# A max-then-softmax attention whose key pieces are compared in pairs: the pairing extended from one third to two thirds of the pieces

## The chip, the core and the metric

The kernel runs on one core of a Trainium2 chip. The metric is the device time of one execution in microseconds. A TensorE clock of 1.00 in the profile is its full 2.4 GHz, 0.50 is 1.2 GHz.

## What is computed

Two attention layers over a 48 x 48 picture with 384 channels, batch 2, 12 heads of 32 channels. The first layer attends to a 7 x 7 neighbourhood, the second to all 2304 positions with a bias by row and by column. Cut to the second layer, which the change touches:

```python
q, k, v = (qkv[0], qkv[1], qkv[2])
q = q * scale
attn = jnp.einsum('bqd,bkd->bqk', q, k)
attn = (attn.reshape(B * nh, H, W, H, W) + rel_h[:, :, :, :, None] + rel_w[:, :, :, None, :]).reshape(B * nh, N, N)
attn = jax.nn.softmax(attn, axis=-1)
out = jnp.einsum('bqk,bkd->bqd', attn, v)
```

Before, in between and after stand the group norms, the projections and the residual sums (`x = x + layer(_gn(x))`).

## The kernel before

**Stages, units, steps.** The second attention is `attention_full`. It has 24 stages, one for each head and batch element. A stage has six units of 384 queries, and a unit has nine steps; a step takes 256 of the 2304 keys (two key tiles of 128). So a stage has 54 steps, and the whole 1296.

**Two passes.** The softmax needs the largest score of each query before the exponentials. A first pass (`max_piece` on TensorE, L1608) makes scores in half precision, with queries on the partitions: for each of a unit's three query tiles, six pieces of 384 keys. The second pass (`scores_of`, L1635 and L1637) makes the scores again with keys on the partitions, the negated maximum added as one more row of the matmul. `exps` (L1760, ScalarE) takes the exponential, `low_part` (L1796) subtracts its upper half to keep the rest as a second half-precision number, and `weighted` (L1662, L1663) multiplies both with the values. `low_part` runs on VectorE for steps 1, 4 and 7 of a unit and on GpSimd for the six others.

**Order.** Each engine runs its own list, written by hand. The first pass runs 12 steps ahead of the second (`AHEAD`): in each step TensorE makes four score matmuls, one piece (call it p0), the weighted sums of the step three before, and a second piece (p1). Two PSUM banks hold the pieces in turn, so a piece waits until the piece two before it has been read. At step 7 of a unit, ahead of the scores, `row_of_max` (L1621) turns the three negated maxima of the coming unit into a row, which `place_row` on ScalarE (L1731) copies beside the queries; it waits for the maxima, and for the reading of the next unit's first piece, since it writes into that bank.

**Rounds.** How a piece pair is read depends on the step (`is_round`). In a plain step VectorE reduces each of the two pieces to its maximum (L1817, `maxima`). In a round step the even piece's matmul gives the difference of two key pieces' scores instead of a score: the constants (`rival_m`) and the key vectors (`rivals`, L1875, on GpSimd, once a stage in step 31) hold the difference in that piece's place. ScalarE copies it with relu (`leads`, L1746), and one VectorE instruction adds the odd piece and takes the maximum over all (L1810: max(a - b, 0) + b is the larger of the two). In a round step TensorE issues p0 between the second and the third score matmul, in a plain step behind the fourth. Before, steps 2, 5 and 8 of a unit are rounds: the last two of a tile's six pieces. After nine steps VectorE reduces the parts of each tile to the negated maximum (L1824).

**Other work between.** ScalarE takes the result's lower part out of PSUM after step 2 (L1716) and writes the normalised result after step 4 (L1724); VectorE adds the two parts after step 3 (L1835, L1836).

Of the kernel before, what the change touches and what calls it, by code (L numbers as in the profile page):

```python
# [15 lines left out]
TOK = SIDE * SIDE  # L16
ALL = B * TOK
HEADS, D = 12, 32
# [15 lines left out]
UNIT = KR * SIDE  # L34
PIECE = 384
PIECES = TOK // PIECE
RIVALS = slice(TOK - 2 * PIECE, TOK - PIECE)
LOWEST = -3.0e38
QT = UNIT // 128
HALO = WINDOW // 2  # L40
# [46 lines left out]
def shape_constants():  # L87

    t = np.arange(TOK)
    strip, row, col = t // STRIP, (t % STRIP) // KC, t % KC  # L90
    one_a = np.zeros((32, TOK + REGS), np.float16)
    for i in range(KC):
        one_a[i, :TOK] = one_a[KC + i, :TOK] = col == i
    one_b = np.zeros((B_ROWS, NA + 1, 128), np.float16)
    for a in range(NA):
        for k in range(128):
            one_b[a * KR + k // KC, a, k] = one_b[SIDE + a * KR + k // KC, a, k] = 1
    one_m = np.zeros((2 * SIDE, TOK + REGS), np.float16)
    one_m[t // SIDE, t] = 1
    one_m[SIDE + t % SIDE, t] = 1  # L100
    strip_m = np.zeros_like(one_m)
    strip_m[row, t] = 1
    strip_m[SIDE + strip * KC + col, t] = 1
    rival_m = strip_m.copy()
    rival_m[:, RIVALS] -= strip_m[:, RIVALS.stop:RIVALS.stop + PIECE]
    pos = np.arange(SIDE)
    start = np.clip(pos - HALO, 0, SIDE - WINDOW)
    outside = ~((pos[:, None] >= start[None]) & (pos[:, None] < start[None] + WINDOW))
    far = np.where(outside, -BIG, 0.0).astype(np.float16)
    far_row = far[:, t // SIDE]  # L110
    far_col = far[:, t % SIDE]
    mask_a = np.zeros((32, NS, TOK), np.float16)
    for c in range(NS):
        mask_a[:KC, c] = far_col[c * KC:(c + 1) * KC]
    mask_b = np.concatenate([far_row, np.zeros_like(far_row)])
    by_strip = row * SIDE + strip * KC + col
    mask_m = np.concatenate([far_row, far_col])[:, by_strip]
    ones_row = np.zeros((B_ROWS, NA + 1, 128), np.float16)
    ones_row[M_ROW] = 1
    group = np.arange(C) // (C // GROUPS)  # L120
    share = (group[:, None] == group[None]).astype(np.float32) / (C // GROUPS)
    share = share.reshape(CT, 128, C).transpose(1, 0, 2).copy()
    spread = (np.arange(2 * HEADS)[:, None] % HEADS == np.arange(C)[None] % HEADS) / INV_SCALE
    spread = spread.astype(np.float16).reshape(2 * HEADS, CT, 128)
    big = np.float16(BIG)
    return {
        "one_a0": one_a * big, "one_a1": one_a, "one_b0": one_b * big + ones_row,
        "one_b1": one_b + ones_row, "one_m0": one_m * big, "one_m1": rival_m,
        "mask_a": mask_a, "mask_b": mask_b, "mask_m": mask_m, "share": share, "spread": spread,
        "ident": np.eye(128, dtype=np.float16),  # L130
    }
# [1266 lines left out]
def attention_full(nc, ctx, x, dram, sem):  # L1398


    PAIRS = TILES // 2
# [7 lines left out]
    STEP_PIECES = 2  # L1409
    UNIT_PIECES = STEP_PIECES * PAIRS  # L1410
    ROUNDS = PIECES // 2
    PARTS = PIECES - 1
    AHEAD = PAIRS + 3
    ROW_STEP = 7
    RIVALS_STEP = 4 * PAIRS - 5
# [71 lines left out]

    def is_round(m):

        return m % ROUNDS == ROUNDS - 1  # L1490

    def rounds(g, m):

        return g * QT + m % PAIRS // ROUNDS + 1

    def row_of(n, k):

# [20 lines left out]
    with nc.Block() as block:  # L1518
# [189 lines left out]
        @block.scalar  # L1708
        def _(act):
            def banked(a):  # L1710
                return out_acc[:, a % 2, 0:QT * VW].rearrange("p (t n) -> p t n", t=QT)

            def take_lo(n, a):

                act.wait_ge(prob_used, n * STEPS + (a + 1) * PAIRS)
                nc.scalar.activation(out_lo[:, a % 2], banked(a)[:, :, 0:D], ACT.Identity).then_inc(lo_copied, 1)  # L1716

            def normalise(h, b, a):

                act.wait_ge(sum_ready, (h * B + b) * NA + a + 1)  # L1720
                if a == 0 and due(h):
                    act.wait_ge(result_out[b], h * RESULT)
                for t in range(QT):
                    nc.scalar.activation(result[:, b, a * QT + t, :], out_sum[:, a % 2, t, :], ACT.Identity,  # L1724
                                         scale=inverse[:, a % 2, t:t + 1]).then_inc(placed, 1)


            def place_row(n, u, b):

                act.wait_ge(row_ready, n * NA + u + 1)  # L1730
                nc.scalar.activation(q_b[M_ROW:M_ROW + 1, b, u * UNIT:(u + 1) * UNIT],  # L1731
                                     max_acc[M_ROW:M_ROW + 1, u % 2, 0:UNIT], ACT.Identity).then_inc(row_copied, 1)

            act.wait_ge(first_in, FIRST)
            nc.scalar.activation(warm[:, :], ident[0:1, 0:1], ACT.Exp)
            def leads(n, m):


                u = m // PAIRS
                g = n * NA + u  # L1740
                j = 2 * (m % PAIRS)
                done = rounds(g, m)
                act.wait_ge(bank_filled, g * UNIT_PIECES + j + 1)
                if due(done - 2):
                    act.wait_ge(bank_read, (done - 3) // QT * UNIT_PIECES + ((done - 3) % QT + 1) * PIECES)
                nc.scalar.activation(lead[:, done % 2, :], max_acc[:, piece_bank(g, u, j), 0:PIECE],  # L1746
                                     ACT.Relu).then_inc(lead_ready, 1)

            for m in range(AHEAD):
                if m - AHEAD + PAIRS == ROW_STEP:  # L1750
                    place_row(0, 0, 0)
                if is_round(m):
                    leads(0, m)

            def exps(n, k):
                free = n * STEPS + k - RING + 1
                act.wait_ge(score_ready, n * STEPS + k + 1)
                if due(free):
                    act.wait_ge(prob_used, free)
                nc.scalar.activation(prob[:, (n * STEPS + k) % RING, :].rearrange("p (j n) -> p j n", j=2),  # L1760
                                     scores[:, 2 * (k % 2):2 * (k % 2) + 2, 0:UNIT], ACT.Exp).then_inc(prob_ready, 1)

            def stage(h, b):
                n = h * B + b
                for k in range(STEPS):
                    coming = row_of(n, k)
                    if coming:
                        place_row(*coming, b if coming[1] else 1 - b)
                    later = ahead(n, k)
                    if later and is_round(later[1]):  # L1770
                        leads(*later)
                    exps(n, k)
                    u, rest = divmod(k - LAG, PAIRS)
                    if rest == PAIRS - 1:
                        if u >= 0:
                            take_lo(n, u)
                        elif not is_first(n):
                            take_lo(n - 1, NA + u)
                    if rest == 1:
                        if u >= 1:  # L1780
                            normalise(h, b, u - 1)
                        elif not is_first(n):
                            normalise(h - (1 - b), 1 - b, NA - 1)

            each_stage(act, stage)
            take_lo(STAGES - 1, NA - 1)
            normalise(HEADS - 1, 1, NA - 1)
# [13 lines left out]
        def _(dve):  # L1801
            def maxima(n, m):
# [3 lines left out]
                if is_round(m):  # L1806
# [3 lines left out]
                    nc.vector.tensor_tensor_reduce(  # L1810
                        out=winner[:, done % 2, :], in0=max_acc[:, piece_bank(g, u, first + 1), 0:PIECE],
                        in1=lead[:, done % 2, :], scale=1.0, scalar=LOWEST, op0=ALU.add, op1=ALU.max,
                        accum_out=part_max[:, u % 2, first // PIECES, PARTS - 1:PARTS]).then_inc(bank_read, 2)
                else:
                    for j in range(first, first + STEP_PIECES):
                        dve.wait_ge(bank_filled, g * UNIT_PIECES + j + 1)
# [48 lines left out]
        @block.gpsimd  # L1865
        def _(pool):
            nc.gpsimd.memset(neg_max[:, :, :], 0.0).then_inc(neg_clear, 1)
            nc.gpsimd.memset(zeros[:, :], 0.0).then_inc(zeros_ready, 1)

            def rivals(h, b):  # L1870


                pool.wait_ge(max_in[b], (h + 1) * MAX)
                ours = k_m[0:D, b, RIVALS]
                nc.gpsimd.tensor_tensor(ours, ours, k_m[0:D, b, RIVALS.stop:RIVALS.stop + PIECE],  # L1875
                                        ALU.subtract).then_inc(rivals_ready, 1)

            rivals(0, 0)

            def stage(h, b):  # L1880
                n = h * B + b
                for k in range(STEPS):
                    if k == RIVALS_STEP and not is_last(n):
                        rivals(h + b, 1 - b)
                    low_part(nc.gpsimd, n, k, low_by_pool)

            each_stage(pool, stage)
# [248 lines left out]
```

## Time and profile before

| | before |
|---|---|
| median of 3 runs | 3177.81 us (3173.26 to 3178.23) |
| profiled execution, its own time | 3173.97 us |
| span of its trace | 3172.2 us |
| TensorE, weight loads, VectorE, ScalarE, GpSimd busy in the span | 2850.6, 1862.6, 2427.4, 2027.8, 1741.1 us |
| mean granted TensorE clock | 0.959 |

A profile is one execution. Durations are read from its trace, and instants are microseconds from the span's start. An instruction's start is recorded; the end of a matmul is modelled, and matmuls overlap in the pipeline, so starts say more about TensorE than busy time does. On VectorE and ScalarE the next instruction can start a little before the recorded end of the one ahead of it. An idle time is put down to the engine whose semaphore came last.

### The profile page before, as it was taken

What the parts mean: (1) busy time and instruction counts of PE and PEld (TensorE: products, weight loads), DVE (VectorE), ACT (ScalarE), POOL (GpSimd) and SP (SyncE); (2) the same over time, 40 slices, a digit from 0 to 9 for tenths busy, and PEclk for the clock granted to TensorE, in tenths of its full rate; (3) what the DMA queues carried; (4) which work ended last, traced back from release to release, by engine and by line L of the source; (5) the groups of instructions that cost most, each with busy time, mean ns of one, the idle gap of its engine ahead of it and who ended that gap; (6) DMA issues with size and microseconds to landing.
All of it is one profiled execution on the core that took longest, in us unless ns stands there. A gap on an engine that the chain in (4) does not pass through costs nothing. (4 is left out here: it accounts for less than half of the span.)

```text
span 3172.2 us, 84223 instructions
## 1 busy us (share of the span) xinstructions
PE 2850.6 (90%) x34200; PEld 1862.6 (59%) x34200; DVE 2427.4 (77%) x5315; ACT 2027.8 (64%) x3866; POOL 1741.1 (55%) x1441
## 2 busy tenths in 40 slices
PE   3895999997669974999999999999999999999977
PEld 2453777774335531666666666666666666666654
DVE  6754888785666533888888888888888888888854
ACT  3433676664334432777777777777777777777764
POOL 3452555552020021777777777777777777777762
PEclk9996999998889986999999999999999999999989
DMA  3426555555526857333332222222222223333115
GB/s 144 157 91 143 141 140 138 137 138 157 199 76 195 225 135 202 66 62 55 64 57 52 52 52 52 52 52 52 52 52 52 52 52 59 63 62 58 23 43 150
DMA packets 219847, 302.00 MB, mean 95 GB/s; under 512 B 134394, under 2 KB 172884, under 8 KB 213972
## 3 DMA queue, kind: packets, MB, share of 16 engines
q1 hardware_dynamic: 219460, 296.62, 38.4%
q8 instruction: 270, 4.42, 0.6%
q14 instruction: 117, 0.96, 0.1%
HBM read 196.56 MB, written 92.64 MB: 91 GB/s over the span
## 5 line engine op out<-in xcount | busy, mean ns | idle before, releaser
L1796 POOL TENSOR_TENSOR fprob_low<-fprob 128x768 f16<-128x768 f32 x864 | 1251.0, 1469 | 547.6 <-ACT fprob L1760 547.6
L1760 ACT ACTIVATE fprob<-fscores 128x768 f32<-128x768 f32 x1296 | 1048.6, 809 | 277.2 <-PE fscores L1637 240.2
L1817 DVE TENSOR_REDUCE fpart_max<-fmax_acc 128x1 f32<-128x384 f32 x1728 | 919.1, 557 | 240.9 <-PE fmax_acc L1608 199.2
L1608 PE MATMUL fmax_acc<-fk_m,fq_m 128*128 128x384 f16 x2592 | 845.3, 327 | 30.2 <-DMA fident<-in_ident 27.3
L1635 PE MATMUL fscores<-fq_a,fk_a 128*128 128x384 f16 x2592 | 842.1, 325 | 10.8 <-DMA fk_m<-in_one_m 10.8
L1637 PE MATMUL fscores<-fq_b,fk_b 97*128 97x384 f16 x2592 | 846.9, 327 | 0.0
L1662 PE MATMUL fout_acc<-fv,fprob 128*128 128x65 f16 x7776 | 610.4, 191 | 3.0 <-POOL fprob_low L1796 2.4
L1663 PE MATMUL fout_acc<-fv,fprob_low 128*128 128x33 f16 x7776 | 593.4, 178 | 1.2 <-issue 1.2
L1662 PEld LDWEIGHTS fout_acc<-fv,fprob 128*128 128x128 bf16 x7776 | 541.2, 97 | 90.4 <-POOL fprob_low L1796 3.7
L1663 PEld LDWEIGHTS fout_acc<-fv,fprob_low 128*128 128x128 f16 x7776 | 486.5, 96 | 78.4 <-issue 1.4
L1796 DVE TENSOR_TENSOR fprob_low<-fprob 128x768 f16<-128x768 f32 x432 | 426.4, 987 | 5.9 <-ACT fprob L1760 5.9
L1135 POOL TENSOR_TENSOR prob_low<-prob 128x242 f16<-128x242 f32 (+2 forms) x360 | 249.8, 716 | 257.6 <-ACT prob L1093 255.4
L1608 PEld LDWEIGHTS fmax_acc<-fk_m,fq_m 128*128 128x128 f16 x2592 | 251.0, 97 | 189.6 <-DVE fpart_max L1817 99.7
L1637 PEld LDWEIGHTS fscores<-fq_b,fk_b 97*128 97x128 f16 x2592 | 250.7, 97 | 162.8 <-issue 0.5
L1635 PEld LDWEIGHTS fscores<-fq_a,fk_a 128*128 128x128 f16 x2592 | 251.3, 97 | 69.2 <-DMA fk_m<-in_one_m 11.2
L1746 ACT ACTIVATE flead<-fmax_acc 128x384 f32<-128x384 f32 x432 | 210.0, 486 | 109.1 <-PE fmax_acc L1608 109.1
L1810 DVE CUSTOM_DVE_ANT_0 fwinner<-fmax_acc,flead 128x384 bf16<-128x384 f32 x432 | 240.9, 558 | 13.2 <-PE fmax_acc L1608 2.7
L1153 DVE TENSOR_REDUCE tile_max<-max_acc 128x1 f32<-128x282 f32 (+3 forms) x432 | 176.7, 436 | 77.7 <-PE max_acc L921 76.8
L1074 ACT ACTIVATE x<-out_acc 32x384 f32<-32x384 f32 (+1 forms) x288 | 138.8, 482 | 129.8 <-PE out_acc L982 126.1
L1093 ACT ACTIVATE prob<-scores 128x266 f32<-128x266 f32 (+1 forms) x576 | 188.4, 407 | 45.4 <-PE scores L943 41.4
L942 PE MATMUL scores<-q_a,k_a 128*128 128x57 f16 (+4 forms) x1296 | 175.2, 225 | 29.9 <-DMA q_b<-max_row 28.2
L470 PE MATMUL acc<-x,w_hi 128*128 128x384 f16 (+1 forms) x441 | 150.5, 343 | 56.2 <-POOL x L324 29.1
(138 smaller groups left out, 4266.4 us busy)
## 6 DMA issues: line engine op xcount, KB each, us to landing
q_a<-q_hi SPq DMA_DIRECT2D x48, 432.0 KB, 5.8
fq_a<-q_hi SPq DMA_DIRECT2D x48, 432.0 KB, 7.8
q_a<-q_lo SPq DMA_DIRECT2D x24, 432.0 KB, 7.5
row_bias<-bias_slot SPq DMA_DIRECT2D x24, 432.0 KB, 7.3
col_bias<-bias_slot SPq DMA_DIRECT2D x72, 144.0 KB, 4.8
fq_a<-q_lo SPq DMA_DIRECT2D x24, 432.0 KB, 8.7
fq_a<-col_bias SPq DMA_DIRECT2D x24, 432.0 KB, 17.0
fq_b<-row_bias SPq DMA_DIRECT2D x24, 432.0 KB, 5.8
```

Of the source, the lines that this page charges most:

```text
L1093: nc.scalar.activation(dst, src, ACT.Exp).then_inc(prob_ready, 1)
L1135: last = engine.tensor_tensor(prob_low[0:p, k % RING, cut], prob[0:p, k % RING, cut], prob[0:p, k % RING, :].bitcast(BF16)[:, 1::2][:, cut ...
L1608: nc.tensor.matmul(max_acc[:, piece_bank(g, u, j), 0:PIECE], q_m[:, b, tile * 128:(tile + 1) * 128], k_m[:, b, piece * PIECE:(piece + 1) * ...
L1635: nc.tensor.matmul(bank, k_a[:, b, tile * 128:(tile + 1) * 128], q_a[:, b, tile // NA, a * UNIT:(a + 1) * UNIT], start=True, stop=False)
L1637: last = nc.tensor.matmul(bank, k_b[:, tile % NA], q_b[:, b, a * UNIT:(a + 1) * UNIT], start=False, stop=True)
L1662: nc.tensor.matmul(dst, high[:, cut], v[:, b, tile, :], start=False, stop=False)
L1663: last = nc.tensor.matmul(dst[:, D:VW], low[:, cut], v[:, b, tile, D:VW], start=False, stop=(tile == TILES - 1 and t == QT - 1))
L1746: nc.scalar.activation(lead[:, done % 2, :], max_acc[:, piece_bank(g, u, j), 0:PIECE], ACT.Relu).then_inc(lead_ready, 1)
L1760: nc.scalar.activation(prob[:, (n * STEPS + k) % RING, :].rearrange("p (j n) -> p j n", j=2), scores[:, 2 * (k % 2):2 * (k % 2) + 2, 0:UNI ...
L1796: engine.tensor_tensor(prob_low[:, slot, :], prob[:, slot, :], prob[:, slot, :].bitcast(BF16)[:, 1::2], ALU.subtract).then_inc(done, 1)
L1810: nc.vector.tensor_tensor_reduce(out=winner[:, done % 2, :], in0=max_acc[:, piece_bank(g, u, first + 1), 0:PIECE], in1=lead[:, done % 2, : ...
L1817: nc.vector.reduce_max(part_max[:, u % 2, j // PIECES, j % PIECES:j % PIECES + 1], max_acc[:, piece_bank(g, u, j), 0:PIECE], axis=AX.X).th ...
```

## The change

In the second layer steps 1, 2, 4, 5, 7 and 8 of a unit become rounds; steps 0, 3 and 6 stay plain. Of a tile's six pieces the first two are still reduced one by one, pieces 2 and 3 and pieces 4 and 5 are compared as differences. The constants hold two difference pieces, the subtraction on GpSimd covers two pieces of 384 keys in one instruction, and a tile has four partial maxima, not five. The wait of a lead for its buffer follows the new count of rounds. The diff in full:

```diff
-RIVALS = slice(TOK - 2 * PIECE, TOK - PIECE)
+RIVALS = (2 * PIECE, 4 * PIECE)
...
     rival_m = strip_m.copy()
-    rival_m[:, RIVALS] -= strip_m[:, RIVALS.stop:RIVALS.stop + PIECE]
+    for at in RIVALS:
+        rival_m[:, at:at + PIECE] -= strip_m[:, at + PIECE:at + 2 * PIECE]
...
     ROUNDS = PIECES // 2
-    PARTS = PIECES - 1
+    PARTS = PIECES - 2
...
     def is_round(m):
 
-        return m % ROUNDS == ROUNDS - 1
+        return m % ROUNDS > 0
 
     def rounds(g, m):
 
-        return g * QT + m % PAIRS // ROUNDS + 1
+        return (g * QT + m % PAIRS // ROUNDS) * (ROUNDS - 1) + m % ROUNDS
...
                 if due(done - 2):
-                    act.wait_ge(bank_read, (done - 3) // QT * UNIT_PIECES + ((done - 3) % QT + 1) * PIECES)
+                    tiles, pair = divmod(done - 3, ROUNDS - 1)
+                    act.wait_ge(bank_read, tiles * PIECES + 2 * (pair + 2))
...
-                        accum_out=part_max[:, u % 2, first // PIECES, PARTS - 1:PARTS]).then_inc(bank_read, 2)
+                        accum_out=part_max[:, u % 2, first // PIECES, 1 + m % ROUNDS:2 + m % ROUNDS]).then_inc(bank_read, 2)
...
                 pool.wait_ge(max_in[b], (h + 1) * MAX)
-                ours = k_m[0:D, b, RIVALS]
-                nc.gpsimd.tensor_tensor(ours, ours, k_m[0:D, b, RIVALS.stop:RIVALS.stop + PIECE],
+                ours = k_m[0:D, b, RIVALS[0]:TOK].rearrange("p (i s n) -> p i s n", s=2, n=PIECE)
+                nc.gpsimd.tensor_tensor(ours[:, :, 0], ours[:, :, 0], ours[:, :, 1],
                                         ALU.subtract).then_inc(rivals_ready, 1)
```

## Rows read from the trace of the kernel before

**Rows 1.** Busy us (instructions) of PE, PEld, DVE, ACT, POOL in a stretch; clock, DMA.

```profile
1700.00:2700.00 1000.00, 979.36 (x13236) 659.89 (x13235) 879.50 (x1914) 764.38 (x1357) 711.89 (x493) 1.00 0.29 55
```

**Rows 2.** Waits, 1258 to 3040 us: waiter <- releaser: us in total, times, longest.

```profile
PE fmax_acc L1621 <- DVE fpart_max L1817: 35.1, 142, 0.4
...
PE fscores L1635 <- DMA fk_m<-in_one_m: 10.8, 1, 10.8
```

**Rows 3.** Timeline of TensorE, steps 5 to 7: start, us, line, out<-in [idle before].

```profile
2006.11 0.32 PE L1635 MATMUL fscores<-fq_a,fk_a 128*128 128x384 f16 x1
...
2006.44 0.33 PE L1608 MATMUL fmax_acc<-fk_m,fq_m 128*128 128x384 f16 x1
...
2007.27 0.32 PE L1608 MATMUL fmax_acc<-fk_m,fq_m 128*128 128x384 f16 x1
2007.43 0.32 PE L1635 MATMUL fscores<-fq_a,fk_a 128*128 128x384 f16 x1
...
2008.09 0.33 PE L1608 MATMUL fmax_acc<-fk_m,fq_m 128*128 128x384 f16 x1
...
2009.16 0.33 PE L1621 MATMUL fmax_acc<-fident,fneg_max 128*128 128x128 f16 x3 [0.25 <-DVE fpart_max L1817]
2009.32 0.33 PE L1635 MATMUL fscores<-fq_a,fk_a 128*128 128x384 f16 x1
```

**Rows 4.** Timeline of VectorE over the same steps (x2: two in a row).

```profile
2006.78 0.95 DVE L1796 TENSOR_TENSOR fprob_low<-fprob 128x768 f16<-128x768 f32 x1
2007.77 0.56 DVE L1810 CUSTOM_DVE_ANT_0 fwinner<-fmax_acc,flead 128x384 bf16<-128x384 f32 x1
...
2008.45 1.05 DVE L1817 TENSOR_REDUCE fpart_max<-fmax_acc 128x1 f32<-128x384 f32 x2
```

**Rows 5.** Timeline of ScalarE over steps 4 and 5 of that unit.

```profile
2005.65 0.81 ACT L1760 ACTIVATE fprob<-fscores 128x768 f32<-128x768 f32 x1 [0.59 <-PE fscores L1637]
2006.36 0.73 ACT L1724 ACTIVATE fresult<-fout_sum,finverse 128x32 f32<-128x32 f32 x3
2006.99 0.47 ACT L1746 ACTIVATE flead<-fmax_acc 128x384 f32<-128x384 f32 x1
2007.36 0.80 ACT L1760 ACTIVATE fprob<-fscores 128x768 f32<-128x768 f32 x1
```

**Rows 6.** Timeline of ScalarE and VectorE ahead of the first step.

```profile
1235.55 0.49 ACT L1746 ACTIVATE flead<-fmax_acc 128x384 f32<-128x384 f32 x1 [2.73 <-PE fmax_acc L1608]
1236.17 0.56 DVE L1810 CUSTOM_DVE_ANT_0 fwinner<-fmax_acc,flead 128x384 bf16<-128x384 f32 x1 [0.75 <-ACT flead L1746]
...
1236.65 0.55 DVE L1817 TENSOR_REDUCE fpart_max<-fmax_acc 128x1 f32<-128x384 f32 x1
```

**Rows 7.** Timeline of VectorE in the first steps of the first stage.

```profile
1262.97 0.95 DVE L1796 TENSOR_TENSOR fprob_low<-fprob 128x768 f16<-128x768 f32 x1
1263.84 0.55 DVE L1810 CUSTOM_DVE_ANT_0 fwinner<-fmax_acc,flead 128x384 bf16<-128x384 f32 x1
```

**Rows 8.** All of line L1875: duration in ns, shortest/median/longest, first and last start.

```profile
L1875 POOL TENSOR_TENSOR fk_m<-fk_m x24: 897/1622/1626, 1230.2 to 2960.5; 32x384 f16<-32x384 f16 x24
```

**Rows 9.** Timeline of TensorE, VectorE, GpSimd around one L1875 (p1 of step 31 first).

```profile
2056.20 0.32 PE L1608 MATMUL fmax_acc<-fk_m,fq_m 128*128 128x384 f16 x1
...
2057.04 0.96 DVE L1796 TENSOR_TENSOR fprob_low<-fprob 128x768 f16<-128x768 f32 x1
...
2057.14 1.62 POOL L1875 TENSOR_TENSOR fk_m<-fk_m 32x384 f16<-32x384 f16 x1
```

**Rows 10.** Timeline of VectorE and GpSimd where their subtractions start almost together.

```profile
733.38 0.37 DVE L1135 TENSOR_TENSOR prob_low<-prob 128x209 f16<-128x209 f32 x1
733.38 1.05 POOL L1135 TENSOR_TENSOR prob_low<-prob 16x384 f16<-16x384 f32 x1
...
3058.04 1.46 POOL L1796 TENSOR_TENSOR fprob_low<-fprob 128x768 f16<-128x768 f32 x1
...
3058.12 2.19 DVE L1796 TENSOR_TENSOR fprob_low<-fprob 128x768 f16<-128x768 f32 x1 [1.14 <-ACT fprob L1760]
```

## The prediction: which instants move, and what waits on them

> **What bounds the kernel now.** I read the second attention alone, because the diff touches nothing else. The busy time by stretch comes first. In 1000 us of its steady part TensorE is busy 979 us at a granted clock of 1.00, VectorE 880, ScalarE 764, GpSimd 712 [rows 1]. So TensorE is the bound, and the question is only where it stands still. The list of waits answers: inside the loop only the row of maxima (L1621) waits, for the reductions of L1817, 142 times, once for each unit of nine steps [rows 2]. The 35 us there are too few, since the view lets each matmul end late; starts are safer. So the timeline gives the size. Call a step's class its number modulo 9 and S5 the start of the first score matmul of class 5; p0 and p1 are the two key-piece matmuls of a step. S5 to S6 is 1.32 us with no gap between matmuls; S6 to S7 is 1.89 us [rows 3]. The row's own matmuls need 0.16 (2009.16 to 2009.32), so 1.89 - 1.32 - 0.16 = 0.41 us per unit is standstill, 59 us over 143 units. A unit is 8 x 1.32 + 1.89 = 12.5 us, and the 144 units are 1800 of the span's 3172 us. The 59 us are all that any relief of VectorE could give back. It hangs on p0 of class 6: its matmul starts at S6+0.66, its reduction 0.36 later, takes 0.55, and the row starts 0.16 after that [rows 3, 4, 6].
>
> **What goes and what comes.** Of each tile's six pieces, pieces 2 and 3 change from two reductions to one copy with relu on ScalarE and one add-and-maximum on VectorE; 432 pairs in all. VectorE loses two reductions that start 0.50 apart (two take 1.05, one 0.55) and gains one custom instruction that holds it 0.48 (1236.17 to 1236.65) [rows 4, 6]: 432 x 0.5 = 216 us less work. ScalarE gains 432 leads, each of which holds it 0.37 (2006.99 to 2007.36) [rows 5]: 160 us. In a unit of 12.5 us that lifts ScalarE's share from 76% to about 88% and lowers VectorE's from 88% to about 80%. TensorE issues the same matmuls; in a class 1, 4 or 7 step p0 moves ahead of the second pair of scores, from S+0.66 to S+0.33, which costs nothing: a step of the old order and one of the new are both 1.32. So neither throughput limits; only instants can. The maximum over 12 parts in place of 15 and the different constant mask are worth nothing that a row could show. The work ahead of the first step changes by a few instructions, but the first scores then wait 10.8 us for a load [rows 2], which covers it; without that cover it would be some 2 us, once.
>
> **The row.** The reduction of p0 in class 6 stands behind class 5's custom instruction and the unit's maximum. Before, that instruction started 0.50 after its p1 matmul (2007.27 to 2007.77), so at S5+1.66, and not because of the subtraction ahead of it: one such instruction followed 0.87 behind a subtraction (1262.97 to 1263.84), which would have been 2007.65 here [rows 3, 4, 7]. Now there are two new routes to it. By VectorE: class 4 is a round too, its custom instruction starts at S4+1.16+0.50 = S4+1.66, the subtraction behind it 0.48 later, at S4+2.14 = S5+0.82, the next custom instruction 0.87 later: S5+1.69. By ScalarE: lead of class 4 at S4+0.33+0.36 (taken as for a reduction), exponential 0.37 later, results 0.71 after that (2005.65 to 2006.36), 0.63 for three of them, so the lead of class 5 starts at S4+2.40 = S5+1.08, takes 0.47, and a custom instruction started 0.13 after a lead's end (1235.55+0.49 to 1236.17): S5+1.68 [rows 5, 6]. Both say 0.03 later than before. Then 0.68 over the unit's maximum to the reduction (2007.77 to 2008.45) [rows 4]: S6+1.05 where it was S6+1.02, and the row is late by the same 0.03: 143 x 0.03 = 4.3 us. Bounds: 0, if the custom instruction still waits for p1 alone, and 0.11, if the subtraction holds VectorE for its whole 0.95 (0.08 more): 0 to 16 us.
>
> **The other new waits.** A p1 must find the custom instruction two pieces back finished. That takes 0.56 from its start and 0.16 to TensorE, so class 6 gets p1 free at S5+1.69+0.72 = S6+1.09 against the 1.16 at which it is due; classes 0 and 3 have the same or more (class 3 also starts an accumulation). Class 7's p0 now comes at S7+0.33 and needs both reductions of class 6: the second ends about S6+2.1, and S7 is S6+1.92; it fits by about 0.01. The lead of class 7 stands behind the row's copy on ScalarE, exponentials of round steps end about 0.2 later than now, and scores ask for them only two steps on; GpSimd, idle 288 of 1000 us [rows 1], loses idle time alone when its inputs come 0.2 later. All this I cost at nothing. Ends: nothing, or, if each handoff is 0.1 longer than the rows, about 0.15 per unit, 20 us.
>
> **The subtraction on GpSimd.** Once a stage GpSimd makes the difference in the keys (L1875), in the class 4 step 31, 23 times inside the loop. It now covers 768 elements per partition, not 384. Alone the old one took 0.90; in the loop 1.62 [rows 8], because VectorE's subtraction had started 0.10 ahead of it (2057.04, 2057.14) [rows 9]: of these two, one runs and the other waits. When VectorE comes second it pays: 2.19 in place of 0.95 [rows 4, 10]. The new length has no row; a GpSimd subtraction of 768 elements takes 1.46 [rows 10], twice 0.90 is 1.79, and 0.90 is the lower end; I take 1.46, the row with the same element count. Now the instants. GpSimd's start stays at p1+0.94 (2056.20 to 2057.14); VectorE's moves from 2057.04, p1+0.84, to p1+0.50+0.48, p1+0.98 [rows 4, 6, 9]. So VectorE comes 0.04 after it, no longer 0.10 before.
> If VectorE still gets through first, GpSimd waits 0.72+0.14 and then runs 1.46, to about S5+3.1. Its next two subtractions run to S5+6.0, into VectorE's subtraction of class 7 at S7+2.14 = S5+5.4. That one is late by about 0.45 (in [rows 10] an overlap of 1.38 cost 1.24, so 0.6 costs 0.45), the custom instruction behind it ends at S0+1.38, class 0's p1 goes at S0+1.54 and not S0+1.16: 0.38 x 23 = 8.7 us.
>
> **Sum.** 4.3 + 8.7 = 13.0 us over the profiled execution's 3174.0 gives 3187.0. The median of the runs shown, 3177.8, lies 3.8 above that execution, so the forecast is 3190.8 us.
>
> **Rivals.**
> GpSimd gets through first. In [rows 10] VectorE started within 0.01 of GpSimd and won (its 0.37 for 209 elements, against 0.95 for 768, holds no wait; GpSimd's 1.05, against the 0.90 that 384 elements take in [rows 8], does), and elsewhere started 0.08 after it and lost. 0.04 lies in the middle. The loss would be 1.28 (1.24, plus 0.04 for the earlier arrival); it moves class 5's custom instruction to S5+2.97 and the row with it: 23 x 1.31 + 120 x 0.03 = 33.7 us, 3211.5; with 0.90 or 1.79 as length 3198 or 3219. The Trainium skill, page SBUF — State Buffer, section "SBUF: two separate sides", says that the port pair which the two engines share is an exclusive lock for a whole instruction and goes to the one that starts first. By that rule this rival holds in every stage; the 2.19 in [rows 10] agrees that the loser stands still, and the pair at 733.38 leaves open who counts as first.
> Not slower: the difference on GpSimd takes under about 1.0 us for its 768 elements. Then, VectorE being first, GpSimd's queue is through before class 7's subtraction, the 8.7 us fall away, and with 0 to 0.03 at the row the time is 3178 to 3182. For it: 32 partitions and 16-bit inputs only. Against it: 384 elements took 0.90, 0.6 of the 1.46 for 768.
> Faster: VectorE's 216 us less work shorten the standstill of 0.41. For it: the reduction at 2008.45 starts just when VectorE comes free. Against it: it also starts just when its matmul allows, and the chain to it gets longer, not shorter. A quarter of 59 us would be 3163.
> The handoffs are tighter than the rows: every unit loses 0.15, and with the 13.0 above the time is about 3212.
>
> **How the numbers follow.** Forecast 0.40; GpSimd first 0.31; not slower 0.16; tight handoffs 0.08; faster 0.05. The forecast is 3191. Range 3175 to 3222: from no effect, a little below the median, to GpSimd first with the long length and some of the handoff loss. A measurement of this kernel tells about 0.2% (6.4 us) from no change. Faster 0.05; same 0.16 and a share of 0.06 of the forecast, whose row term may be nothing: 0.22; slower 0.73.
>
> **What would show it.** VectorE's busy share in the steady part at about 80%, ScalarE's at 88%, TensorE's hardly changed. S6 to S7 at 1.92 in ordinary units. At L1875, once a stage: VectorE's subtraction near 0.95 and the difference above 2 us (forecast), or the subtraction at 2.2 and the row 1.3 late (rival). If steps other than class 6 lengthen in every unit, the handoffs were wrong; if S6 to S7 falls below 1.89, I misread what the row waits for.

## The result: 3213.0 us, 1.2% slower

| | before | after |
|---|---|---|
| median of 4 runs each | 3175.53 us (3171.35 to 3178.23) | 3213.00 us (3208.67 to 3213.88) |
| ratio, 95% interval | | 1.0120 (1.0108 to 1.0132) |
| profiled execution, span | 3173.97, 3172.2 us | 3212.84, 3211.1 us |
| VectorE, ScalarE busy in the span | 2427.4, 2027.8 us | 2207.6, 2182.5 us |

The forecast was 3191 us, the rival "GpSimd gets through first" 3211.5. First the steady part by busy time (columns as in [rows 1]) and the two waits of TensorE for VectorE inside the loop (as in [rows 2], 1258 to 3080 us), both of after:

```profile
1700.00:2700.00 1000.00, 960.50 (x12965) 659.00 (x12964) 740.82 (x1873) 831.22 (x1562) 707.01 (x483) 1.00 0.28 54
```

```profile
PE fmax_acc L1622 <- DVE fpart_max L1819: 43.5, 142, 0.4
...
PE fmax_acc L1609 <- DVE fpart_max L1812: 26.0, 23, 1.1
```

VectorE falls from 880 to 741 us and ScalarE rises from 764 to 831, the clock is 1.00 as before, and TensorE's busy time falls by 19 us of every 1000 all the same. The second wait is new: 23 times, once a stage, a key piece (L1609) waits 1.1 us for a custom instruction (L1812). The line of GpSimd's difference in after, to set beside [rows 8] (ns, shortest/median/longest):

```profile
L1877 POOL TENSOR_TENSOR fk_m<-fk_m x24: 1624/1632/1634, 1233.4 to 2998.2; 32x768 f16<-32x768 f16 x24
```

It never waits: alone or in the loop it takes 1.63. So VectorE must. The timeline of VectorE, GpSimd and TensorE around one step 31, as in [rows 9]; p1 of step 31 starts it, 2076.62 is the start of step 33, 2079.97 that of step 34:

```profile
2075.14 0.32 PE L1609 MATMUL fmax_acc<-fk_m,fq_m 128*128 128x384 f16 x1
...
2075.64 0.56 DVE L1812 CUSTOM_DVE_ANT_0 fwinner<-fmax_acc,flead 128x384 bf16<-128x384 f32 x1 [0.67 <-PE fmax_acc L1609]
2076.12 2.40 DVE L1798 TENSOR_TENSOR fprob_low<-fprob 128x768 f16<-128x768 f32 x1
2078.44 0.54 DVE L1812 CUSTOM_DVE_ANT_0 fwinner<-fmax_acc,flead 128x384 bf16<-128x384 f32 x1
...
2076.07 1.63 POOL L1877 TENSOR_TENSOR fk_m<-fk_m 32x768 f16<-32x768 f16 x1
2077.67 2.18 POOL L1798 TENSOR_TENSOR fprob_low<-fprob 128x768 f16<-128x768 f32 x1
...
2076.62 0.32 PE L1636 MATMUL fscores<-fq_a,fk_a 128*128 128x384 f16 x1
...
2079.05 0.34 PE L1609 MATMUL fmax_acc<-fk_m,fq_m 128*128 128x384 f16 x1 [1.12 <-DVE fpart_max L1812]
2079.81 0.33 PE L1622 MATMUL fmax_acc<-fident,fneg_max 128*128 128x128 f16 x3 [0.42 <-DVE fpart_max L1819]
2079.97 0.33 PE L1636 MATMUL fscores<-fq_a,fk_a 128*128 128x384 f16 x1
```

The difference starts at p1+0.93, VectorE's subtraction at p1+0.98, as worked out (the lines are rounded; in the 23 stages VectorE comes 0.038 to 0.047 us later). VectorE's then takes 2.40 in place of 0.95, the custom instruction behind it and the row are late, and step 33 lasts 3.35 us. The starts of the first score matmul of all steps give the account. Step 33 has a median of 1.89 before and 3.36 after, the five other class 6 steps of a stage 1.89 and 1.93, and every other class keeps its median to within 0.004. That is 23 x 1.47 + 120 x 0.040 = 33.8 + 4.8 = 38.6 us, against 38.9 in the span. The loop also starts 2.5 us later, and the other steps and the tail together take as much less; the start differs by some us between executions.

### The profile page after: what moved, and what is told of

The parts are those of the page before. It is cut to its first block and busy times, and to the rows that moved or that the text cites. A ratio compares the mean times of both kernels' runs of the same rounds, so it can differ in the third digit from the quotient of the medians.

```text
span 3211.1 us, 85519 instructions
## 1 busy us (share of the span) xinstructions
PE 2856.0 (89%) x34200; PEld 1887.4 (59%) x34200; DVE 2207.6 (69%) x5315; ACT 2182.5 (68%) x4298; POOL 1758.6 (55%) x1441
## 3 DMA queue, kind: packets, MB, share of 16 engines
q14 instruction: 127, 1.04, 0.1%
## 5 line engine op out<-in xcount | busy, mean ns | idle before, releaser
L1798 POOL TENSOR_TENSOR fprob_low<-fprob 128x768 f16<-128x768 f32 x864 | 1268.1, 1489 | 565.9 <-ACT fprob L1762 565.9
L1762 ACT ACTIVATE fprob<-fscores 128x768 f32<-128x768 f32 x1296 | 1034.4, 809 | 76.5 <-PE fscores L1638 55.7
L1609 PE MATMUL fmax_acc<-fk_m,fq_m 128*128 128x384 f16 x2592 | 845.4, 327 | 56.8 <-DVE fpart_max L1812 29.0
L1812 DVE CUSTOM_DVE_ANT_0 fwinner<-fmax_acc,flead 128x384 bf16<-128x384 f32 x864 | 479.7, 555 | 446.8 <-PE fmax_acc L1609 445.9
L1748 ACT ACTIVATE flead<-fmax_acc 128x384 f32<-128x384 f32 x864 | 424.4, 491 | 154.9 <-PE fmax_acc L1609 118.7
L1819 DVE TENSOR_REDUCE fpart_max<-fmax_acc 128x1 f32<-128x384 f32 x864 | 458.4, 555 | 65.4 <-PE fmax_acc L1609 37.1
L1798 DVE TENSOR_TENSOR fprob_low<-fprob 128x768 f16<-128x768 f32 x432 | 450.4, 1043 | 5.7 <-ACT fprob L1762 5.7
L1609 PEld LDWEIGHTS fmax_acc<-fk_m,fq_m 128*128 128x128 f16 x2592 | 251.1, 97 | 190.7 <-DVE fpart_max L1812 34.5
```

What stands on the lines that cost most here:

```text
L1609: nc.tensor.matmul(max_acc[:, piece_bank(g, u, j), 0:PIECE], q_m[:, b, tile * 128:(tile + 1) * 128], k_m[:, b, piece * PIECE:(piece + 1) * ...
L1798: engine.tensor_tensor(prob_low[:, slot, :], prob[:, slot, :], prob[:, slot, :].bitcast(BF16)[:, 1::2], ALU.subtract).then_inc(done, 1)
L1812: nc.vector.tensor_tensor_reduce(out=winner[:, done % 2, :], in0=max_acc[:, piece_bank(g, u, first + 1), 0:PIECE], in1=lead[:, done % 2, : ...
L1819: nc.vector.reduce_max(part_max[:, u % 2, j // PIECES, j % PIECES:j % PIECES + 1], max_acc[:, piece_bank(g, u, j), 0:PIECE], axis=AX.X).th ...
```

## Experiments

The theory of the order: of VectorE's subtraction and GpSimd's difference the first makes the other wait, the change puts GpSimd ahead by 0.04 us, and this costs 34 of the 39 us. Its rival, the theory of the length: a difference of 768 elements costs TensorE its time wherever it stands.

**GpSimd comes later.** A wait in GpSimd's list:

```diff
                     if k == RIVALS_STEP and not is_last(n):
+                        pool.wait_ge(low_by_dve, lows(n, k)[0])
                         rivals(h + b, 1 - b)
```

> The changed kernel with a wait: GpSimd starts the difference only when VectorE's subtraction of step 31 is done. Theory of the order: VectorE's subtraction takes 0.95, the difference 1.63 undisturbed but 1.0 us later, step 33 is 1.93 again, and step 36 longer by about 0.75 (GpSimd's next two subtractions run into VectorE's of step 34): 3175.5 + 6 + 17 = 3198 us. Theory of the length: 3213 us or more, since GpSimd only starts later.

Measured 3197.5 us, 1.0076 (1.0055 to 1.0096). VectorE's subtraction of step 31 takes 0.96 and GpSimd's difference still 1.63, 1.04 us later; step 33 is at 1.92, step 36 at 1.98 in place of 1.32. VectorE and GpSimd in step 31, then VectorE's subtraction of step 34:

```profile
2072.36 0.96 DVE L1798 TENSOR_TENSOR fprob_low<-fprob 128x768 f16<-128x768 f32 x1
...
2073.40 1.63 POOL L1877 TENSOR_TENSOR fk_m<-fk_m 32x768 f16<-32x768 f16 x1 [1.04 <-DVE fprob_low L1798]
...
2076.92 1.77 DVE L1798 TENSOR_TENSOR fprob_low<-fprob 128x768 f16<-128x768 f32 x1
```

A later start of the same instruction takes the loss from 1.20% to 0.76%. The order theory holds, and so does its price for the late queue (0.66 us, 0.75 expected).

Next a pause on GpSimd, first tiny, then of 195 elements, ahead of the difference:

```diff
+                nc.gpsimd.memset(pause[:, :], 0.0)
                 ours = k_m[0:D, b, RIVALS[0]:TOK].rearrange("p (i s n) -> p i s n", s=2, n=PIECE)
```

> The changed kernel with one tiny GpSimd instruction (a memset of one element per partition into a spare tile, about 0.1 us) ahead of each difference in the keys. Theory of the order (whichever of the two subtractions comes first makes the other wait): the difference now starts about 0.05 us behind VectorE's subtraction of step 31 and not 0.04 us ahead of it; VectorE's takes 0.95 again and the difference about 2.4; step 33 falls from 3.36 us to 1.93. GpSimd's queue then runs into VectorE's subtraction of step 34, which is late by about 0.67, and step 36 gets about 0.6 longer: 3175.5 + 6 (the 0.041 us in each unit) + 14 = 3195 us. Theory of the length (a difference twice as long costs TensorE its own extra time wherever it stands): 3213 us or a little more, and VectorE's subtraction of step 31 still 2.4 us.

Measured 3211.1 us, 1.0128 (1.0112 to 1.0145): a miss. The difference starts 0.05 us behind the start of the pause, which takes 0.10; the two overlap on GpSimd:

```profile
2070.67 0.10 POOL L1877 MEMSET fpause<- 128x1 f16 x1
2070.72 1.63 POOL L1879 TENSOR_TENSOR fk_m<-fk_m 32x768 f16<-32x768 f16 x1
...
2070.74 2.44 DVE L1799 TENSOR_TENSOR fprob_low<-fprob 128x768 f16<-128x768 f32 x1
```

GpSimd is still ahead by about 0.01 us (0.007 to 0.012 in the 23 stages; the lines are rounded) and goes first; this run doesn't tell the theories apart. The longer pause does:

> The changed kernel with a longer idle instruction (a memset of 195 elements per partition into a spare tile; 0.26 us for this size in the trace of before) on GpSimd ahead of each difference. With the tiny one the difference started 0.01 us ahead of VectorE's subtraction and kept its turn. Theory of the order: the difference now comes about 0.18 behind VectorE's subtraction, which takes 0.95 to 1.1; step 33 is 1.93, step 36 longer by about 0.7; 3175.5 + 6 + 16 = 3198 us. Rival, a queue of GpSimd instructions is not broken between two of them: VectorE's subtraction, 0.04 behind the memset, waits for memset and difference, 2.6 us long; step 33 about 3.6 and 3218 us.

Measured 3190.0 us, 1.0038 (1.0024 to 1.0053).

```profile
2066.16 0.26 POOL L1877 MEMSET fpause<- 128x195 f16 x1
...
2066.22 0.95 DVE L1799 TENSOR_TENSOR fprob_low<-fprob 128x768 f16<-128x768 f32 x1
...
2066.37 2.29 POOL L1879 TENSOR_TENSOR fk_m<-fk_m 32x768 f16<-32x768 f16 x1
```

Now VectorE is 0.15 us ahead, takes 0.95, and GpSimd pays 0.66. Step 33 is 1.92 and step 36 1.77. Idling GpSimd for 0.26 us once a stage, with nothing else changed, takes the loss from 1.20% to 0.38%. The memset, under way when VectorE's subtraction starts, costs VectorE nothing.

**The length alone, in the kernel before.** Here VectorE is 0.10 us ahead. In the first of two kernels GpSimd makes an unused difference of 768 elements, and VectorE the real one in step 34:

```diff
+                nc.gpsimd.tensor_tensor(unused[0:D], ours[:, :, 0], ours[:, :, 1], ALU.subtract).then_inc(unused_done, 1)
...
+                    if k == RIVALS_STEP + 3 and not is_last(n):
+                        own_rivals(h + b, 1 - b)
```

> The kernel before, in which GpSimd makes an unused difference of 768 elements at step 31 (into a spare tile) and VectorE the real one of 384 in step 34. VectorE's subtraction of step 31 still starts 0.10 us ahead of GpSimd's difference. Theory of the order: VectorE's takes 0.95, the difference about 2.36, step 33 stays at 1.89; GpSimd's queue runs into VectorE's subtraction of step 34, and step 36 is longer by about 0.4: 3175.5 + 10 = 3185 us. Theory of the length: step 33 at about 3.3, 3175.5 + 33 = 3208 us.

Measured 3216.4 us, 1.0144 (1.0128 to 1.0159), a time that neither theory gave. Step 33 stays at 1.89, as the order theory has it for a difference of 768 elements behind VectorE, but step 35 goes from 1.32 to 3.18. What cost the time was the experiment's own instruction on VectorE in step 34, 0.35 us alone. It waited not for one GpSimd instruction but for two in a row:

```profile
2001.71 2.88 POOL L1798 TENSOR_TENSOR fprob_low<-fprob 128x768 f16<-128x768 f32 x2
...
2001.92 2.88 DVE L1846 TENSOR_TENSOR fk_m<-fk_m 32x384 f16<-32x384 f16 x1
```

The next run leaves VectorE's list alone and puts a second, unused difference of 384 elements behind the real one:

```diff
+                nc.gpsimd.tensor_tensor(unused[0:D], k_m[0:D, b, PIECE:2 * PIECE], k_m[0:D, b, 2 * PIECE:3 * PIECE],
+                                        ALU.subtract)
```

> The kernel before with a second, unused difference of 384 elements on GpSimd (into a spare tile) right behind the real one of step 31; nothing more on VectorE, which in the run before this one had met GpSimd in step 34 with an instruction of the experiment's own. VectorE's subtraction of step 31 still starts 0.10 us ahead of GpSimd. Theory of the order: it takes 0.95, step 33 stays at 1.89; GpSimd is busy some 2.5 us there, its two next subtractions meet VectorE's of step 34, and step 36 is longer by about 0.5: 3175 + 12 = 3187 us. Theory of the length: as much GpSimd work there as in the changed kernel costs 33 us: 3208 us, and step 33 grows.

Measured 3191.0 us, 1.0038 (1.0024 to 1.0053).

```profile
2068.09 0.96 DVE L1797 TENSOR_TENSOR fprob_low<-fprob 128x768 f16<-128x768 f32 x1
...
2068.19 1.62 POOL L1876 TENSOR_TENSOR fk_m<-fk_m 32x384 f16<-32x384 f16 x1
2069.78 0.90 POOL L1878 TENSOR_TENSOR funused<-fk_m 32x384 f16<-32x384 f16 x1
```

Step 33 is 1.89, step 36 1.80: as much GpSimd work in the same place, here as two instructions, costs 11 us (23 x 0.48) behind VectorE, and the mechanism is the forecast's, not the rival's. With the later start, the longer pause and step 33 of the kernel above, all with one instruction of 768 elements, the length theory falls.

**Half the length in the changed kernel.** GpSimd makes one difference, VectorE the other in step 34:

```diff
-                nc.gpsimd.tensor_tensor(ours[:, :, 0], ours[:, :, 0], ours[:, :, 1],
+                nc.gpsimd.tensor_tensor(ours[:, 0, 0], ours[:, 0, 0], ours[:, 0, 1],
                                         ALU.subtract).then_inc(rivals_ready, 1)
```

> The changed kernel with GpSimd making only one of the two differences in step 31 (384 elements) and VectorE the other in step 34. Theory of the order: GpSimd still comes 0.04 us first, but for 0.90 and not 1.63, so VectorE's subtraction of step 31 takes 2.40 - 0.73 = 1.67 and step 33 3.36 - 0.73 = 2.63 us. If the length of the difference does not set the loss, both stay at 2.40 and 3.36.

Measured 3197.7 us (one run).

```profile
2070.88 1.68 DVE L1801 TENSOR_TENSOR fprob_low<-fprob 128x768 f16<-128x768 f32 x1
...
2070.83 0.91 POOL L1889 TENSOR_TENSOR fk_m<-fk_m 32x384 f16<-32x384 f16 x1
```

Step 33 has a median of 2.63. With a difference shorter by 0.73 us, VectorE's subtraction and step 33 are shorter by 0.73 each: once GpSimd is first, the loss follows the difference's length one to one.

**No difference on GpSimd.** VectorE makes both in step 34 (`nc.vector` for `nc.gpsimd`, `RIVALS_STEP = 4 * PAIRS - 2`).

> The changed kernel with the difference made by VectorE in step 34, where it stands idle for 1.5 us, and none on GpSimd. Both theories: the 34 us of step 33 go. What it tells apart is the rest: if the remaining loss is the 0.041 us of each unit (class 6 at 1.93, 143 times), the time is 3175.5 + 6 = 3181 us; if VectorE's relief is worth anything by itself, it comes out below 3175 us here.

Measured 3179.7 us (median of 10 runs, 3173.0 in 13 of before): 1.0020 (1.0008 to 1.0033). All six class 6 steps have a median of 1.92, the other classes keep theirs. VectorE's relief is in full (745 of 1000 us busy), the collision is gone, and the kernel is still no faster than before. What remains is the forecast's first term.

**The 0.04 us of an ordinary unit.** The timeline of after, as in [rows 3 to 5]; S5 is 2012.52 and S6 2013.84:

```profile
2012.52 0.32 PE L1636 MATMUL fscores<-fq_a,fk_a 128*128 128x384 f16 x1
...
2013.34 0.95 DVE L1798 TENSOR_TENSOR fprob_low<-fprob 128x768 f16<-128x768 f32 x1
2014.22 0.56 DVE L1812 CUSTOM_DVE_ANT_0 fwinner<-fmax_acc,flead 128x384 bf16<-128x384 f32 x1
...
2014.91 1.01 DVE L1819 TENSOR_REDUCE fpart_max<-fmax_acc 128x1 f32<-128x384 f32 x2
...
2013.61 0.49 ACT L1748 ACTIVATE flead<-fmax_acc 128x384 f32<-128x384 f32 x1
...
2015.60 0.33 PE L1622 MATMUL fmax_acc<-fident,fneg_max 128*128 128x128 f16 x3 [0.29 <-DVE fpart_max L1819]
```

The custom instruction starts at S5+1.70, 0.88 behind the subtraction and 0.12 behind the lead's end: both routes of the forecast meet. Moving the three results behind the next exponential takes ScalarE's route away:

```diff
-                    if rest == 1:
+                    if rest == 2:
                         if u >= 1:
                             normalise(h, b, u - 1)
```

> The changed kernel with ScalarE's three results (L1725) after the exponential of class 5 and not of class 4, which takes 0.63 us off ScalarE's route to the lead of class 5. If the 0.041 us of an ordinary unit come by VectorE (custom instruction, subtraction, custom instruction: 0.48 + 0.88 behind the first), class 6 stays at 1.92 to 1.93; if they come by ScalarE's lead, it falls to 1.89. Step 33 stays near 3.36 by either.

The ordinary class 6 steps have a median of 1.906, between the two answers: VectorE's route alone brings 0.016 of the 0.040, the lead's the rest. But the kernel took 3326.0 us (one run), and step 33 6.32 us. VectorE's subtraction of step 31 waits for three GpSimd instructions (here the exponential of class 5, which feeds the second of them, stands between):

```profile
2040.46 1.64 POOL L1877 TENSOR_TENSOR fk_m<-fk_m 32x768 f16<-32x768 f16 x1
...
2040.50 5.26 DVE L1798 TENSOR_TENSOR fprob_low<-fprob 128x768 f16<-128x768 f32 x1
...
2040.76 0.80 ACT L1762 ACTIVATE fprob<-fscores 128x768 f32<-128x768 f32 x1
...
2042.06 2.88 POOL L1798 TENSOR_TENSOR fprob_low<-fprob 128x768 f16<-128x768 f32 x2
```

This exponential ends at 2041.56, 0.5 us before the difference does. In after the same one comes later:

```profile
2076.76 0.81 ACT L1762 ACTIVATE fprob<-fscores 128x768 f32<-128x768 f32 x1
```

It ends at 2077.57, 0.13 before the difference's end at 2077.70, and VectorE gets in between the two GpSimd instructions: the second then takes 2.18. That ScalarE's lateness is what kept the loss at 1.47 us a stage isn't shown. In the kernel without a difference on GpSimd, VectorE's own in step 34 (0.55 us alone) gets in between two GpSimd instructions although the second one's input was ready 0.84 us before the end of the first (2065.61, 2066.45):

```profile
2064.80 0.81 ACT L1762 ACTIVATE fprob<-fscores 128x768 f32<-128x768 f32 x1
...
2064.98 1.47 POOL L1798 TENSOR_TENSOR fprob_low<-fprob 128x768 f16<-128x768 f32 x1 [1.53 <-ACT fprob L1762]
...
2065.95 0.90 DVE L1846 TENSOR_TENSOR fk_m<-fk_m 32x768 f16<-32x768 f16 x1
...
2066.40 1.78 POOL L1798 TENSOR_TENSOR fprob_low<-fprob 128x768 f16<-128x768 f32 x1
```

Not all of the 3326 us is VectorE's waiting. In the kernel with the results later TensorE stands still for 3.99 us in step 33, and when it goes on the granted clock has fallen to 0.50 (1.2 GHz). This comes in each of 23 stages; in the loops of the other kernels here the clock stays at 1.00. The matmul that waited, and the stretch around and behind it (columns as in [rows 1]):

```profile
2046.29 0.50 PE L1609 MATMUL fmax_acc<-fk_m,fq_m 128*128 128x384 f16 x1 [3.99 <-DVE fpart_max L1812]
...
2046.00:2052.00 6.00, 5.46 (x40) 3.18 (x41) 2.79 (x8) 2.70 (x5) 0.00 (x0) 0.50 0.01 3
```

Steps 34 and 35 take 2.42 us there in place of 1.32: 23 x 2.2 = 51 us, a third of the 152 us by which the span is longer than before.

**What bounds the row.** The kernel before, with the row of step 7 between the two pairs of scores:

```diff
-                    if coming:
-                        row_of_max(*coming)
...
                     scores_of(n, b, k, 0)
+                    if coming:
+                        row_of_max(*coming)
```

> The kernel before with one move on TensorE: in step 7 of a unit the row of maxima (L1621) goes between the first and the second pair of score matmuls, which don't need it, and not ahead of them. My reading of the row's wait (it hangs on p0 of class 6, 0.41 us of standstill that no relief of VectorE gives back): the row is ready at S6+1.73, the first pair covers S6+1.32 to 1.65, so 0.08 of the 0.41 is left; p0 of class 7 may wait 0.02; classes 6 and 7 together take 2.90 in place of 3.21 us, 143 x 0.31 = 44 us less: 3132 us. If the row's wait were set by something that moves with the row (VectorE or ScalarE being late), the time stays at 3176.

Measured 3130.9 us, 0.9856 (0.9836 to 0.9877): 1.44% or 46 us faster than before. Classes 6 and 7 take 1.32 + 1.56 = 2.88 us, against 1.89 + 1.32. Class 7 in this kernel:

```profile
2002.59 0.32 PE L1635 MATMUL fscores<-fq_a,fk_a 128*128 128x384 f16 x1
2002.99 0.33 PE L1621 MATMUL fmax_acc<-fident,fneg_max 128*128 128x128 f16 x3
2003.16 0.33 PE L1635 MATMUL fscores<-fq_a,fk_a 128*128 128x384 f16 x1
```

Two matmuls need 0.33, so the row waits 0.07 where it waited 0.41. The same move with two thirds of the pieces in rounds, VectorE making the differences, and class 7's p0 back behind the scores (the part of the diff for p0):

```diff
+                    early = is_round(k) and k % PAIRS != ROW_STEP
```

> The changed kernel with the difference made by VectorE in step 34 (as in the earlier run, 6 us above the kernel before), the row moved between the two pairs of scores, and class 7's p0 back behind the second pair, since both reductions of class 6 must be done before it. The row is ready at S6+1.76; classes 6 and 7 together about 2.92 us: 3135 us, so two thirds of the pieces in rounds still no better than one third. If VectorE's lower load were worth something once the row's wait is covered, this kernel would come out below the other of this pair.

Measured 3143.3 us, 0.9891 (0.9873 to 0.9909), 8 us above the 3135 expected. Class 7 has a median of 1.59 in place of 1.56, and class 0 a mean of 1.35 in place of 1.32, since step 36 is late by 0.2 once a stage. Once the row is covered the change still gives nothing; the best kernel here is the one before with the row moved.

## Why the prediction was wrong

- **What bounds the kernel:** right. TensorE stands still only at the row, by 0.41 us, and VectorE's load has no part in it: VectorE 15% less busy brought nothing, the row moved in TensorE's list brought 46 us.
- **The row term:** right in its place and both its routes, and somewhat small: 0.03 us forecast, 0.040 measured, over 143 units 4.3 against 5.7 us.
- **The shares:** VectorE's was forecast at 80% and ScalarE's at 88%; after has 74% and 83%, the kernel without the collision 75% and 84%. The prediction's own 216 and 160 us over the loop's 1800 are 12 and 9 points, which gives 76% and 85%. Nothing in the forecast's time hangs on them.
- **The other handoffs at nothing:** right; all classes but 6 kept their lengths in after.
- **The step that failed: "If VectorE still gets through first".** The instants were right (VectorE 0.04 behind forecast, 0.04 measured), but between the rows at 0.01 and 0.08 the forecast gave the pair to VectorE. GpSimd had it in all 23 stages. The row it leaned on, the pair at 733.38, comes from other forms in another stage of the program, and VectorE's subtraction there is the second of two in a row, the first still running when GpSimd's starts. Where the same two come 0.03 us apart, in the kernel without a difference on GpSimd, VectorE's waits (1.02 in place of 0.37; the lines are of before, then of that kernel). The pair was no evidence for this place. Inside the loop GpSimd went first at a lead of only 0.01 us (the tiny pause). So the 8.7 us of that branch never came, and 33.8 us of the rival did.

```profile
733.09 0.66 DVE L1135 TENSOR_TENSOR prob_low<-prob 128x209 f16<-128x209 f32 x2
...
736.80 1.02 DVE L1136 TENSOR_TENSOR prob_low<-prob 128x209 f16<-128x209 f32 x1
...
736.77 0.82 POOL L1136 TENSOR_TENSOR prob_low<-prob 16x384 f16<-16x384 f32 x1
```

- **The rival's price:** 1.31 us a stage forecast, 1.47 measured. The mis-sized part is the difference's length, 1.46 taken from a row of the same element count, 1.63 measured. That its 3211.5 lies so near the 3213.0 is in part luck: its 33.7 us are 4 to 5 short, and the median that they were added to, of three runs, was 2.3 above that of the four. The lower end that the "not slower" rival needed (under 1.0) was far off.
- **The branch itself was priced well:** where experiments put VectorE first, step 36 was longer by 0.45, 0.66 and 0.48 us, forecast 0.38 with the shorter length.
- **The rule cited from the Trainium skill** (page SBUF — State Buffer, section "SBUF: two separate sides": the first to start holds the shared ports for its whole instruction) gave the right answer inside the loop at leads of 0.01, 0.04, 0.10 and 0.15 us. The kernels above add that the port can also go from one GpSimd instruction to the next past a waiting VectorE.
- **Left open:** why VectorE kept the turn at 733.38 (that its first subtraction still held the port is a guess), and what decides whether a GpSimd instruction follows the one ahead past a waiting VectorE. Its input was ready 0.13 us early in after and 0.84 in the kernel without a difference on GpSimd, both with VectorE in between, and 0.5 us early in the kernel with the results later, without: that time alone doesn't decide.

## What to carry to other kernels

Ahead of a relief for a busy engine, find the one instant at which the bounding engine waits, and ask whether the relief moves it; here moving the waiting instruction behind work that doesn't need it gave what the relief could not. When an edit shifts a two-input VectorE instruction by a tenth of a microsecond, list the GpSimd instructions near it and who starts first, before and after: a turned order costs about the length of the instruction that now goes first (here 1.47 us for one of 1.63). If both orders lie within the error of the estimate, neither is a forecast; give GpSimd a wait that fixes the order, or take its instruction off.

## What was not expected of the hardware

A waiting VectorE subtraction isn't always let in when the GpSimd instruction ahead of it ends. In one kernel it waited for three in a row, 5.26 us in place of 0.95, and in another for two, 2.88 in place of 0.35; what decides it stays open. After 3.99 us without work TensorE was granted 0.50 of its clock, and its next two steps took 2.42 us in place of 1.32: that wait cost more than its own length. The same difference of 16-bit inputs on 32 partitions took 1.63 us on GpSimd, longer than a subtraction with as many 32-bit elements in each of 128 partitions (1.46).
